# Key and query feature projections of the first layer: two 64-row matmuls per head pair in place of one zero-padded 128-row matmul

## The reference, cut to what matters

```python
def _spherical_features(x, projection):
    x_norm = x / (jnp.linalg.norm(x, axis=-1, keepdims=True) + 1e-08)
    proj = jnp.einsum('bhsd,hfd->bhsf', x_norm, projection)
    return jax.nn.relu(proj) + YAT_EPS                      # 0.1
Q, K, V = heads(x @ Wq + bq), heads(x @ Wk + bk), heads(x @ Wv + bv)
Qp = _spherical_features(Q, projection)
Kp = _spherical_features(K, projection)
KV = jnp.einsum('bhsf,bhsd->bhfd', Kp, V)
QKV = jnp.einsum('bhsf,bhfd->bhsd', Qp, KV)
normalizer = jnp.einsum('bhsf,bhf->bhs', Qp, jnp.sum(Kp, axis=2))
out = QKV / jnp.maximum(normalizer, 1e-06)[..., None]
```

## Time and profile before

| | |
|---|---|
| median of 3 runs | 3582.38 us (3576.8 to 3586.23) |
| profiled execution | span 3585.0 us from first to last instruction; the page has no other time of that execution, so 3585.0 stands for its own time too |
| PE busy | 3130.7 us, 87% of the span |
| PEld busy | 2858.4 us, 80% |
| DVE busy | 2093.7 us, 58% |
| ACT busy | 1289.4 us, 36% |
| mean granted PE clock | 0.929 of full speed |

### The profile page before, as it was taken

One profiled execution on the slowest core, in us unless ns is written; L12 is line 12 of the kernel. 1 busy time (PEld: TensorE's weight loads), 2 busy tenths in 40 slices (PEclk: granted clock), 3 DMA queues, 4 the chain that ended last, 5 costly groups with the idle time before them and its releaser, 6 DMA issues.

```text
span 3585.0 us, 52301 instructions
## 1 busy us (share of the span) xinstructions
PE 3130.7 (87%) x21816; PEld 2858.4 (80%) x21816; DVE 2093.7 (58%) x3678; ACT 1289.4 (36%) x2211; POOL 401.6 (11%) x302
## 2 busy tenths in 40 slices
PE   4999999989969879999569999988998999969990
PEld 4998797579958478898469998888998999968980
DVE  4986377977637734444556655665364734646662
ACT  2453055544411023333234424433144413335550
POOL 0034443432000010000200000000000000011002
PEclk8999999999979889999789999999999999969995
DMA  5422124122023054644541100332221322148875
GB/s 204 135 53 39 1 39 109 1 48 73 15 94 120 12 147 157 190 145 148 174 148 50 36 26 26 110 127 80 84 82 54 105 77 84 66 156 262 266 230 177
DMA packets 283230, 371.98 MB, mean 104 GB/s; under 512 B 45544, under 2 KB 233752, under 8 KB 281192
## 3 DMA queue, kind: packets, MB, share of 16 engines
q1 hardware_dynamic: 169816, 209.50, 18.6%
q0 software_dynamic: 51248, 68.03, 8.0%
q10 hardware_dynamic: 61904, 90.67, 7.2%
HBM read 291.72 MB, written 83.74 MB: 105 GB/s over the span
## 4 chain that ended last, share of the span: by engine, by line
PE 53%; DVE 4%; DMA 3%; issue 2%; ACT 1%; ACTq 1%; POOL 0%; another core or an unknown queue 0%; POOLq 0%; DVEq 0%; SPq 0%
PE PV L430 12%; PE PV L431 11%; PE PV L432 11%; PE PV L534 5%; PE PS L430 3%; PE PS L432 3%; PE PS L431 3%; DMA b<-y_d,gidx 2%; PE PA L565 1%; PE PA L458 1%; ACTq L1490 1%; DVE b L1816 1%; PE PA L850 0%; PE PV L841 0%; PE PV L862 0%
## 5 line engine op out<-in xcount | busy, mean ns | idle before, releaser
L430 PE MATMUL PV<-WH,b_split 128*125 128x256 f32 (+2 forms) x3708 | 1093.9, 295 | 155.7 <-DVE b_split L1602 138.0
L431 PE MATMUL PV<-WH,b_split 128*125 128x256 f32 (+2 forms) x3708 | 1081.4, 292 | 0.0
L432 PE MATMUL PV<-WH,b_split 128*125 128x256 f32 (+2 forms) x3708 | 1079.9, 291 | 0.0
L1602 DVE TENSOR_TENSOR b_split<-b,b_split 128x500 fp32r<-128x500 f32 x1040 | 688.1, 677 | 469.3 <-ACT b_split L1207 454.9
L1207 ACT CAST b_split<-b 128x500 fp32r<-128x500 f32 x1040 | 625.2, 612 | 819.5 <-PE PV L432 723.2
L430 PEld LDWEIGHTS PV<-WH,b_split 128*125 128x125 f32 (+2 forms) x3708 | 707.4, 191 | 181.4 <-issue 122.0
L431 PEld LDWEIGHTS PV<-WH,b_split 128*125 128x125 f32 (+2 forms) x3708 | 709.9, 191 | 10.1
L432 PEld LDWEIGHTS PV<-WH,b_split 128*125 128x125 f32 (+2 forms) x3708 | 706.6, 191 | 11.4
L1585 DVE TENSOR_TENSOR WH<-WS,WH 128x1024 fp32r<-128x1024 f32 x292 | 344.5, 1221 | 154.3 <-ACT WH L1192 153.0
L1192 ACT CAST WH<-WS 128x1024 fp32r<-128x1024 f32 x292 | 291.9, 1050 | 192.2 <-DMA WS<-in_L_gnn_W_neigh 149.0
L430 PE MATMUL PV<-b_split,WH 128*128 128x250 f32 (+3 forms) x1136 | 336.6, 296 | 8.5 <-DVE b_split L1602 6.4
(11 more groups left out here) (260 smaller groups left out, 3806.5 us busy)
## 6 DMA issues: line engine op xcount, KB each, us to landing
WS<-in_L_ffn_w SPq DMA_DIRECT2D x46, 1024.0 KB, 6.9
WH<-at_d SPq DMA_DIRECT2D x20, 1220.7 KB
WS<-in_L_ffn_gate_w SPq DMA_DIRECT2D x16, 1024.0 KB, 5.5
WS<-in_L_ffn_up_w SPq DMA_DIRECT2D x16, 1024.0 KB, 6.0
WS<-in_L_ffn_down_w SPq DMA_DIRECT2D x16, 1024.0 KB, 5.1
y_d<-b ACTq DMA_DIRECT2D x60, 256.0 KB
y_d<-b ACTq DMA_DIRECT2D x64, 196.0 KB
b<-key_d POOLq DMA_DIRECT2D x4, 2560.0 KB, 9.7
```

Source lines behind the costliest of these rows:

```text
L430: pe.matmul(o, a[0], b[0], start=start, stop=False, **kw)
L431: pe.matmul(o, a[0], b[1], start=False, stop=False, **kw)
L432: return pe.matmul(o, a[1], b[0], start=False, stop=stop, **kw)
L1602: ve.tensor_tensor(lo, src, hi.bitcast(F32), ALU.subtract).then_inc(xl_done, 1)
```

## The change

In the key stage, the one projection matmul over 128 rows and 512 moving columns becomes two, each over the 64 rows of one head and that head's 256 feature columns: the first on rows 0 to 63, the second on rows 64 to 127. Each takes a `PV` bank of its own and uses its first 256 columns, so DVE empties each turn with two instructions of 256 columns, and line 703 waits for two releases per turn.

In the query stage, the projection matmul reads only the 64 rows of its head. The number of matmuls and their columns stay. The order within a step changes from (head, feature half) to (feature half, head), so that even turns (DVE) are the first head's and odd turns (ACT) the second's. The accumulations of turn n-4 still stand between two projections.

The zeros in `proj` stay where they are and are no longer read. Layer 1 of the code (`pbd`) is not touched.

```diff
@@ key stage, PE
-                    pe.matmul(v.take(pe)[0:R, :], cols(B3)[:, pr, i * R:(i + 1) * R], proj[pr],
-                              start=True, stop=True).then_inc(v_full, 1)
+                    for hh in range(2):
+                        rows_of, feats = slice(hh * HD, (hh + 1) * HD), slice(hh * F0, (hh + 1) * F0)
+                        pe.matmul(v.take(pe)[0:R, 0:F0], cols(B3)[rows_of, pr, i * R:(i + 1) * R],
+                                  proj[pr][rows_of, feats], start=True, stop=True).then_inc(v_full, 1)
...
-                    pe.wait_ge(v_free, mark["kp"] + m + 1)
+                    pe.wait_ge(v_free, mark["kp"] + 2 * (m + 1))
@@ query stage, PE
-                    step, hh, f = n // 4, n // 2 % 2, n % 2
+                    step, f, hh = n // 4, n // 2 % 2, n % 2
+                    rows_of = slice(hh * HD, (hh + 1) * HD)
...
-                    if f == 0:
+                    if hh == 0:
                         bank, done = v.take(pe), v_full
...
-                    pe.matmul(bank[:, 0:cn], proj[pr][:, at:at + P], cols(B3)[:, pr, c0:c0 + cn],
+                    pe.matmul(bank[:, 0:cn], proj[pr][rows_of, at:at + P], cols(B3)[rows_of, pr, c0:c0 + cn],
                               start=True, stop=True).then_inc(done, 1)
...
-                    step, hh, f = m // 4, m // 2 % 2, m % 2
+                    step, f, hh = m // 4, m // 2 % 2, m % 2
...
-                    if f == 0:
+                    if hh == 0:
                         pe.wait_ge(v_free, mark["qp"] + m // 2 + 1)
@@ key stage, DVE
-                emptied(ve.tensor_scalar(RB[0:R, n % 4, :], v.read(ve)[0:R, :], 0.0, 0.1, ALU.max, ALU.add))
+                for hh in range(2):
+                    emptied(ve.tensor_scalar(RB[0:R, n % 4, hh * F0:(hh + 1) * F0], v.read(ve)[0:R, 0:F0], 0.0, 0.1,
+                                             ALU.max, ALU.add))
```

## The result

| | |
|---|---|
| median of the changed kernel | 3609.16 us |
| median of the kernel before | 3582.38 us |
| ratio, 95% interval | 1.0076 [1.0058, 1.0094] |
| the same two kernels on another occasion | 3608.37 against 3584.25, 1.0070 [1.0054, 1.0085] |

The change makes the kernel slower by 0.7 to 0.8%, 24 to 27 us, where 12 were forecast. Two of the changed kernel's eleven executions took 3756 and 3741 us, at a mean granted clock of 0.892 and 0.894 where the others have 0.930 to 0.933; they are not in the ratios, and the profile shown here is one of another execution of the same kernel (`after_again`, span 3604.6 us), at the clock of the rest.

The account below looks back on a forecast made before the run. PE was taken to bound the key stage alone and the query stage together with DVE. Key stage 0 plus query stage +12 on the 3582.4 us median gave about 3595 us, range 3560 to 3650.

Parts of the forecast that it names:

- What bounds the two stages: Key stage purely PE's at 143.4 us; query stage shared by PE and DVE at 146.0 us.
- Overlap in the key stage: Key-stage projections: only the middle two of four records overlap, three slots for four, gaining 0.215 us per turn, 17.2 us.
- The switch: Both stages: each change between half-array and full-array matmul costs 0.11 us, one bare weight load; 155 plus 183 of them.
- the prediction's own sign: Query stage: starts 0.81 us apart, stage about 158 us; wrong if it stays at 146 or goes over 165.
- the tail of 0.165: PE: a record is 0.593 us long at a pace of 0.43, leaving a 0.165 us tail, not counted in the forecast.
- In the query stage: No overlap gain; 183 switches lose 20.1 us, 8 of PE's 9.5 us standing are given back, leaving +12.
- The small edits: Double emptying, banks, 160 more records and weight loads, waits and the DVE/ACT swap: nothing, hidden under PE's work.
- Cheap switches: Rival: switches below 0.05 us and heads overlap; key stage gains 0 to 34.4 us, total 3565 or 3548; chance 0.22.
- Dear switches: Rival: the array runs empty at each switch; 3613 with the tail alone, 3649 with tail and load; chance 0.28.
- Nothing happens: Rival: 64-row matmuls cost what padded ones do, halves take turns, switches are free; 3582; chance 0.20.
- The fourth: Rival: granted clock falls to 0.51 for part of both stages, or DVE's emptying sets the turn; +20 to +140; chance 0.03.
- The room at the scatter: Downstream: the scatter's last DMA is issued at 854.3 and first read at 984.8, 130 us of room for gains.

Follow-up runs that it names:

- after_again: The changed kernel run once more with no edit, against the kernel before; ratio 1.0070, median 3608.37 us, profiled execution 3604.6 us.
- The control: Key stage of the change, but both 256-column projections over all 128 rows, with the query stage of the kernel before; ratio 0.9992, median 3580.83 us.
- after: Profile of the changed kernel's execution that took 3756 us, no further edit.
- query_only: Only the query-stage hunks of the change, on the kernel before; ratio 1.0069, median 3607.91 us.
- both_grouped: Half-array projections in both stages, two turns' projections and then two turns' accumulations, against the kernel before; ratio 0.9902, median 3546.95 us.
- paired query stage: Query stage with two heads' half-array projections, then two accumulations; key stage of the kernel before; ratio 0.9999, median 3581.9 us; repeated 1.0005, 3580.45 us.

## Why the prediction was right, and where its sizes were off

**What bounds the two stages: right.** The key stage is PE's, the query stage is shared, and the difference arose in the two stages (24.4 us of the 24 to 27 measured). Two figures of its working are off without weight: the waits of the earlier trace rows are 22 places, not 29, and 0.09 to 0.14 us per switch give 3588 to 3605, not 3585 to 3603.

**Overlap in the key stage: the term was too small.** The prediction took three slots of 0.215 us, on the assumption that the first head's second record must start before the second head's first one. The trace shows two slots: the first records of both heads start together, then the second ones. The gain is 80 x 0.43 = 34 us, its upper end, not 17.2.

**The switch: the term that was mis-sized.** "I take 0.11, one weight load laid bare". Measured are 0.20 in both stages. The bare load is there, and beside it 0.09 to 0.10 in which neither a load nor a matmul begins. By the prediction's own sign this step was wrong: it had the starts of the query stage 0.81 apart and the stage at about 158 us, and called itself wrong "if it goes over 165"; measured are 0.90 and 172.2. The choice went to the one standstill whose size could be read from starts, and took the tail of 0.165 for nothing; the truth lies between the load alone (0.11) and load and tail (0.275). "TensorEngine Tiling (Array Packing)" of the Trainium skill said that a change of tiling mode drains TensorE. The runs agree that the change costs and a change of head alone does not, with 0.20 us as the price here. That TensorE runs empty is not shown: in the query stage the next matmul starts at 641.44 and the record before it ends at 641.51, though that end is modelled.

**The two errors met in the key stage.** 34.4 gained against 155 x 0.20 = 31 lost is -3; the forecast had 17.2 against 17.1, that is 0. The stage measured -1.8 in the changed kernel and -3.7 alone. The number was nearly right there by luck, out of two wrong terms.

**In the query stage nothing met it.** 183 x 0.197 = 36 lost, and 26.2 measured, so some 10 us were given back, the whole of the 9.5 in which PE had stood; the forecast had 20.1 - 8 = 12. That an accumulation between any two projections forbids all overlap was the decisive observation and held: with the projections put next to each other the stage went under that of before.

**The small edits: right.** The control shows two emptyings, a second bank and 160 more records to be free within its interval.

**The rivals.** Cheap switches: their overlap was right, their price wrong. Dear switches: closest; its 3613 with the tail alone came from a smaller overlap and a smaller switch that made up for each other. Nothing happens: wrong, both overlap and switch are real. The fourth, that half the array at work brings the granted clock down to that of the cold start, with +20 to +140 us and a chance of 0.03, came nearer than its chance says: in `after` the query stage takes 316.6 us at 0.50 where `after_again` takes 172.2 at 0.98, its starts 1.68 apart (639.46 and 641.14) in place of 0.90, and the execution is 147 us over the median. The same instructions ran at both levels, so the change doesn't force it; whether it makes it possible is not shown. None of the 69 executions of before and none of the 6 of `query_only`, with the same query stage, had it. The room at the scatter held: even in `both_grouped` its last DMA goes out at 869.6 and its result is first read at 956.7.

**Open.** What the 0.09 beyond the weight load is; where half of the paired query stage's 7 us goes when it stands alone; what moves the mean granted clock from execution to execution; and why the query stage fell to the 1.2 GHz level in `after` with PE almost never standing.

## What to carry to other kernels

Two half-array matmuls are worth having only where they stand next to each other, and each stretch of them is paid with two switches of 0.20 us. Count the switches first: here 0.43 us saved per pair against 0.40 for going there and back is next to nothing, the same pairs in groups of two are a gain, and half-array matmuls dealt out singly between full ones are pure loss. Before speeding up PE, set its step beside the step of the engine that empties it, because a gain ends there. And where a stage and the total disagree by a few us, compare executions of the same mean granted clock before looking for a cause in the kernel: between 0.931 and 0.932 alone lie 2 to 7 us for the kernel before.

## What the runs showed of the hardware that I had not expected

Two fp32 matmuls of the code on different halves, each two records, run with their first records together and then their second ones together, 0.01 us apart in the query stage (661.32 and 661.33, 661.77 and 661.78), though the code names one whole matmul after the other. The Trainium skill, page "TensorE: Matmul & The Clock Gate", Part 3, gives some 4 ns between starts on different row groups; in this case's traces, whose starts are kept to the ns, the fp32 records of the two heads start 6 to 7 ns apart (661.319 and 661.325 us; 403.364 and 403.371 in `after_again`), somewhat more than the page has. And a switch takes more than a bare weight load: 0.20 us, the same between records of 128 and 256 columns (key stage) and of 416 (query stage). Last, a PE in flight for 316.3 of 316.6 us can be at a granted clock of 0.50 throughout (`after`), with the same instructions that run at 0.98 in `after_again`.
